# Attention kernel on one core: a local tile's sixteen exponentials issued as four steps, with the first stage ordered anew

## The chip, the core and the metric

One core of a Trainium2 chip runs the kernel. Its engines work through queues of their own, each strictly in the order in which the program was written, and wait for one another through semaphores: PE (TensorE) multiplies matrices and also transposes tiles, PEld is its weight load, DVE (VectorE), ACT (ScalarE) and POOL (GpSimd) work on elements, SP (SyncE) issues most of the DMAs. The metric is the device time of one execution in microseconds (us), lower is better.

## What is computed

`x` has 2 x 1024 tokens of 512 numbers. After a layer norm, two attentions are added to the input:

```python
xn = layernorm(x)
# local attention: 16 heads of 32, 4 key heads, RMS norm and RoPE on q and k
scores = einsum('bhqd,bhkd->bhqk', q, k) * scale
scores = where(causal | abs(i - j) > 64, -10000, scores)
a = einsum('bhqk,bhkd->bhqd', softmax(scores), v) @ Wo.T + bo
# routed attention: 16 heads of 32, one shared key and value per token,
# picked for each token by the largest of 16 gates; causal, not windowed
b = softmax(where(causal, q2 @ k_shared.T / sqrt(32), -inf)) @ v_shared
out = x + a + b
```

## The kernel before

**Two stages.** The first runs over 8 rounds of 256 tokens (two tiles of 128 each). It makes the projections of a round (`gemm`, L934 and L938) and the whole local attention. The second, from about 400 us on, is the routed attention (`key_scores`, `key_values`, `row_scores` and so on). 

**The plan sets the order.** `make_plan()` writes one list of steps, in the order in which a small model of the machine reaches them, and each engine's program walks through that one list and issues its own part of each step. So where a step stands in the list decides its place in every engine's queue. In the model the products (in *chunks* of three matmuls) are the filler: whenever no chain is due, the next chunk is placed. A chain is a generator; each `yield us, [(engine, us), ...]` says what its step costs on PE and on others, and the chain is due again when these have ended, plus `HOP` (0.2). Costs are booked when the yield is reached, so the model may book two steps on an engine in another order than they have in the list.

**The chain of a local tile** is `attend(m, a)` for round m and tile a. Its steps: `q_t` and `k_t` (transposes of q and k, copied by ACT, L1467 and L1475); `scores` (PE, into the four PSUM banks of `win`, L983 and L988); `maxima` (DVE, `l_max`, L1257); `weights` (ACT, sixteen exponentials from `win` into `p_loc`, L1492, four for each bank); `sums` (DVE, `l_sum` and `l_rec`, L1266 and L1269); `scaled` (POOL, `p_loc`, L1658); four `p_t` steps, one for each quarter of the queries (PE transposes of `p_loc` into one bank of `win`, L998, then an ACT copy to `p_loc_t`, L1501); `values` (PE, `av`, L1010); `attn` (ACT and DVE, `attn_t`, L1509 and L1274); `project` (PE, L1024), whose result DVE adds to `x_res` (L1283).

**The four banks are shared** by neighbouring tiles. The next tile's `scores` fill all four before this tile's `p_t` steps; the transposes of quarter g go to bank g, and may start when the next tile's exponentials have read bank g (`p_exp` counts these four by four). So a tile's `p_t` steps and the next tile's `weights` share ACT at the same time.

**Other names that matter.** `x_t` transposes the next round's input (L905), copied by ACT (L1411) and DVE (L1159, `xt`). `fk_lo` is a small DVE step (L1223, `fk_stack`), which `fk_stack` on PE waits for (L965). `qt` copies a routed-query product out of its bank (ACT L1460, DVE L1249). `q_rms` is POOL's L1610. The last two `qt` chunks (`LAST_CHUNKS`) are kept in the room of `rope_b` and `rope_sq`.

Of the kernel before, what the change touches and what calls it, by code (L numbers as in the profile page):

```python
# [179 lines left out]
def make_plan():  # L180
# [3 lines left out]
    pieces_made = [0]  # L184
    p.turned, p.transposed, p.projected, p.fk_stacked = set(), set(), set(), -1
    p.q_kept, p.av_free, p.rooms = -1, 0.0, False
    p.q_lands = {}

    win_free = [0.0] * HKV

# [118 lines left out]
    def take_q(n, kind, a, freed):  # L309
        do("q_biased", n, a)  # L310
        yield 0, [("V", 0.7)], freed
        do("q_square", n, a)
        p.busy(p.now, ("G", 5.2))
        yield 0, [("A", 0.75)]
        do("q_rms", n, a)
        do("q_rope", n, a)
        yield 0, [("V", 1.1), ("G", 3.6), ("G", 1.6), ("", SLACK)]
        yield from attend(n, a)

    def take_qt(n, kind, c, freed):  # L320
        do("qt", n, c)
        yield 0, [("A", 0.4), ("V", 0.45)], freed
        if c == 0 and n < S // PAIR:
            for _ in range(6):
                yield None
            p.q_kept = n
        if n == ROUNDS - 1 and c in (1, 2):
            quarter = 2 * (c - 1)
            do("q_load", 1, 0, 1, quarter)
            p.q_lands.update({(1, quarter + q): p.now + Q_LANDS for q in range(2)})  # L330

    def attend(m, a):
# [21 lines left out]
        yield 1.6, []  # L354
        do("maxima", m, a)
        yield 0, [("V", 1.75)]
        do("weights", m, a)
        def exps_end(end):
            win_free[:] = [end - 1.1 * (HKV - 1 - g) + HOP for g in range(HKV)]
        yield 0, [("A", 4.4)], exps_end  # L360
        do("sums", m, a)
        yield 0, [("V", 2.0)]
        do("scaled", m, a)
# [51 lines left out]
    def first_maxima():  # L415
# [22 lines left out]
            yield None  # L438
        p.take("tp1", ("max_in_rows", 0), ("r_lo", 0))
        do("max_in_rows", 0, 0)  # L440
        yield 0.11, [("A", 0.27)]
        do("max_low", 0, 0)
        yield 0, [("V", 0.35)]
        for _ in range(15):
            yield None

# [260 lines left out]
def mixed_attention_kernel(nc, counts, x, w_tok, w_qt, w_o, b_qkv, b_o, w_norm, scale, rope, ident, mask, rows, rank,  # L707
# [666 lines left out]
    def scalar_program(e):  # L1374
# [12 lines left out]
        for step, *key in plan.steps:  # L1387
# [94 lines left out]
                             tp1[0:HALVES, 0:2, :], ACT.Copy).then_inc(*M["fk_out"].did(m))  # L1482

            elif step == "weights":
                m, a = key
                lane.wait_ge(*M["s_max"].of((m, a)))
                if m:
                    lane.wait_ge(*M["pt_mm"].of((m - 1, a, QUADS - 1)))
                for g in range(HKV):
                    for quad in range(QUADS):  # L1490
                        n = g * QUADS + quad
                        i = e.activation(p_loc[a][:, g, quad, :], win[:, g, quad * KEYS:(quad + 1) * KEYS], ACT.Exp,  # L1492
                                         bias=l_max[:, a, n:n + 1])
                    i.then_inc(*M["p_exp"].did((m, a, g)))

            elif step == "p_t":
                m, a, quad = key
# [414 lines left out]
```

## Time and profile before

| | us |
|---|---|
| three timed runs | 684.29, 685.91, 686.01 |
| their median | 685.91 |
| span of the profiled execution | 684.4 |
| PE busy in it | 646.0 |
| span without PE busy | 38.4 |

How to read the rows further down. A row of the page's first part is an engine, its busy time, its share of the span and its instructions. A row by stretches gives from:to, its length, then busy time of PE, PEld, DVE, ACT and POOL (instructions in brackets), the granted clock of PE as a share of full speed, the busy share of the DMA engines and GB/s. A row of waits gives who waited, for whom, the total in us, how many times and the longest. A row of the timeline gives start, duration, engine, line, operation, output and input, shapes and how many instructions are merged in it; in square brackets how long the engine had idled before and what released it. Row starts of PE overlap with the end of the row ahead of them, because matmuls are pipelined.

### The profile page before, as it was taken

Reading aid. Unit: us, or ns where it says so; the run is one execution under the profiler, and the core shown is the slowest. Engines: PE = TensorE matmul, PEld = TensorE weight load, DVE = VectorE, ACT = ScalarE, POOL = GpSimd, SP = SyncE. Lnnn points to the kernel's source line nnn. Section 1 sums busy time; section 2 is a strip of 40 time slices with the busy share of each in tenths; the row PEclk is TensorE's granted clock in tenths of the full one; section 3 lists DMA queues with packets and bytes.
Section 4 is the critical chain, followed back from the end, with each engine's and each line's share of the span. In section 5 each row is a group of like instructions: output and inputs, shape, how many; then the busy total and the mean of one; then the engine's idle time right before and its main releaser. Section 6 shows DMA issues by size and latency. Waiting matters only on the chain.

```text
span 684.4 us, 19451 instructions
## 1 busy us (share of the span) xinstructions
PE 646.0 (94%) x7432; PEld 510.2 (75%) x7432; DVE 496.3 (73%) x1328; ACT 362.5 (53%) x906; POOL 442.6 (65%) x368
## 2 busy tenths in 40 slices
PE   3788999999999899999899899999999999999997
PEld 3577888887788688888688667777777777777775
DVE  3956966677678866787676368888888787879454
ACT  4436444472527344445335555556566566656674
POOL 3965764938195735684487267685868777778730
PEclk9979999999999999999999999999999999999999
DMA  8522213231232032222214541321314131402011
GB/s 295 206 59 86 82 38 115 86 98 51 66 102 61 30 112 70 64 70 74 77 32 118 158 142 56 96 64 50 111 49 110 51 106 32 110 28 87 4 33 33
DMA packets 64942, 56.61 MB, mean 83 GB/s; under 512 B 6481, under 2 KB 48849, under 8 KB 64849
## 3 DMA queue, kind: packets, MB, share of 16 engines
q1 hardware_dynamic: 62704, 54.45, 27.2%
q8 instruction: 58, 0.95, 0.6%
q10 hardware_dynamic: 2144, 0.93, 0.5%
q14 instruction: 36, 0.29, 0.1%
HBM read 37.20 MB, written 17.89 MB: 80 GB/s over the span
## 4 chain that ended last, share of the span: by engine, by line
PE 78%; DVE 9%; POOL 4%; ACT 3%; issue 2%; DMA 2%; ACTq 1%; DVEq 0%; POOLq 0%
PE gemm L938 17%; PE s_ps L1047 12%; PE od_ps L1096 11%; PE st_ps L1080 10%; PE gemm L1024 6%; PE od_ps L1110 5%; PE win L998 3%; PE gemm L934 3%; PE win L983 2%; PE s_ps L1119 2%; DMA rope_t<-rope 2%; PE av L1010 2%; DVE l_sum L1266 2%; ACT p_loc L1492 2%; DVE l_max L1257 1%
## 5 line engine op out<-in xcount | busy, mean ns | idle before, releaser
L938 PE MATMUL gemm<-w_tok,xt 128*128 128x512 f32 (+1 forms) x768 | 186.1, 384 | 3.3 <-DVE x_res L1283 0.9
L938 PEld LDWEIGHTS gemm<-w_tok,xt 128*128 128x128 f32 x768 | 131.7, 193 | 28.2 <-issue 1.4
L1318 DVE CUSTOM_DVE_ANT_0 s_ps<-s_ps,x_ln 128x512 f32<-128x512 f32 (+3 forms) x224 | 127.6, 620 | 24.4 <-PE s_ps L1047 24.0
L1047 PE MATMUL s_ps<-k_stack,w_tok 96*128 96x512 f32 (+2 forms) x336 | 101.5, 385 | 0.3 <-DVE x_res L1283 0.3
L1080 PE MATMUL st_ps<-w_tok,k_stack 98*128 98x512 f32 x288 | 99.0, 413 | 0.2 <-ACT p_loc L1540 0.2
L1540 ACT ACTIVATE p_loc<-st_ps 128x512 f32<-128x512 f32 x144 | 77.7, 599 | 36.0 <-PE st_ps L1080 34.8
L1634 POOL TENSOR_TENSOR rope_b<-qkv,sin_t 128x128 f32<-128x128 f32 (+1 forms) x32 | 27.5, 880 | 79.5 <-DVE qkv L1232 79.3
L1047 PEld LDWEIGHTS s_ps<-k_stack,w_tok 96*128 96x128 f32 x336 | 55.0, 188 | 28.3 <-DVE picked_fk L1318 12.4
L1492 ACT ACTIVATE p_loc<-win,l_max 128x96 f32<-128x96 f32 x256 | 60.9, 391 | 19.1 <-DVE l_max L1257 19.0
L934 PE MATMUL gemm<-xt,w_qt 128*128 128x256 f32 x384 | 57.1, 293 | 6.3 <-DVE picked_fv L1211 3.5
L1540 ACT ACTIVATE p_loc_t<-st_ps 128x512 f32<-128x512 f32 x96 | 52.4, 599 | 19.8 <-PE st_ps L1080 19.3
L1318 DVE CUSTOM_DVE_ANT_0 s_ps<-s_ps,x_ln,picked_fk 128x128 f32<-128x128 f32 (+3 forms) x112 | 56.8, 556 | 7.5 <-PE s_ps L1047 7.1
L1658 POOL TENSOR_TENSOR p_loc<-p_loc,l_rec 128x1536 f32<-128x1536 f32 x16 | 44.1, 2757 | 26.9 <-DVE l_rec L1269 26.9
L1610 POOL TENSOR_TENSOR rms_y<-rms_v,minus_half 128x20 f32<-128x20 f32 x16 | 58.6, 3665 | 3.3 <-DVE rms_v L1242 2.8
L934 PEld LDWEIGHTS gemm<-xt,w_qt 128*128 128x128 f32 x384 | 50.6, 194 | 10.2 <-DVE picked_fv L1211 4.5
L1024 PE MATMUL gemm<-w_o,attn_t 128*128 128x512 f32 x192 | 54.8, 414 | 3.2 <-DVE attn_t L1274 2.4
L1080 PEld LDWEIGHTS st_ps<-w_tok,k_stack 98*128 98x128 f32 x288 | 50.5, 189 | 9.0 <-ACT p_loc L1540 2.1
L1318 DVE DVE_READ_ACCUMULATOR2_ANT picked_fk<- 128x1 f32 x336 | 47.8, 142 | 0.0
L1501 ACT ACTIVATE p_loc_t<-win 96x512 f32<-96x512 f32 x64 | 36.8, 634 | 16.6 <-PE win L998 16.5
L1096 PE MATMUL od_ps<-p_loc,v_all 128*32 128x128 f32 x1152 | 44.3, 277 | 0.0
L1024 PEld LDWEIGHTS gemm<-w_o,attn_t 128*128 128x128 f32 x192 | 34.1, 193 | 10.0 <-issue 3.2
L1676 POOL TENSOR_SCALAR_AFFINE_SELECT p_loc<-p_loc 128x512 f32<-128x512 f32 x40 | 25.0, 634 | 24.8 <-ACT p_loc L1540 24.8
(172 smaller groups left out, 1298.7 us busy)
## 6 DMA issues: line engine op xcount, KB each, us to landing
w_tok<-q_parts SPq DMA_DIRECT2D x72, 128.0 KB, 2.6
q_parts<-qt SPq DMA_DIRECT2D x120, 64.0 KB
x_ln<-x SPq DMA_DIRECT2D x8, 512.0 KB, 4.7
x_res<-x SPq DMA_DIRECT2D x16, 256.0 KB, 2.9
partial<-x_res SPq DMA_DIRECT2D x16, 256.0 KB, 2.6
w_tok<-partial SPq DMA_DIRECT2D x8, 512.0 KB, 5.2
raw<-w_tok SPq DMA_DIRECT2D x3, 1024.0 KB, 12.9
v_win<-v_rows SPq DMA_DIRECT2D x64, 48.0 KB, 2.2
```

Source lines behind the costliest of these rows:

```text
L934: i = e.matmul(g[:, 0:PAIR], w_qt_p[r][:, k, a * P:(a + 1) * P], xs[l][:, k, :], start=first, stop=last)
L938: i = e.matmul(g[:, 0:cols], xs[l][:, k, a * P:(a + 1) * P], w_tok_p[r][:, k, c0:c0 + cols], start=first, stop=last)
L1024: i = e.matmul(gemm[bank][:, :], attn_t[l][:, kc, :], w_o_p[r][:, kc, :], start=kc == 0 and q == 0, stop=kc == KC - 1 and q == 2)
L1047: e.matmul(s_ps[bank][:, 0:cols], q_op[b][0:HALVES, i, h, :], k_stack[0:HALVES, b * S + c0:b * S + c0 + cols], start=True, stop=True).then ...
L1080: e.matmul(st_ps[k % ST_BANKS][:, :, :], k_stack[0:HALVES + 2, b * S + j * P:b * S + (j + 1) * P], q_op[b][0:HALVES + 2, i, :, :], start=T ...
L1096: mm = e.matmul(od_ps[h * DK:(h + 1) * DK, 0, :], v_all[:, b * IT + j, 0:DK], p_t[k % RING][:, h, :], start=i == j, stop=ends_row(k))
L1318: e.tensor_tensor_reduce(out=s[:, 0:cols], in0=s[:, 0:cols], in1=causal[:, S - width + c0:S - width + c0 + cols], scale=1.0, scalar=dst if ...
L1492: i = e.activation(p_loc[a][:, g, quad, :], win[:, g, quad * KEYS:(quad + 1) * KEYS], ACT.Exp, bias=l_max[:, a, n:n + 1])
L1501: e.activation(p_loc_t[quad][0:KEYS, :, :].rearrange("p g q -> p (g q)"), win[0:KEYS, quad, :], ACT.Copy).then_inc(*M["p_t_r"].did((m, a, ...
L1540: e.activation(p_t[k % RING][:, :, :], st_ps[k % ST_BANKS][:, :, :], ACT.Exp, scale=ROUTED_SCALE).then_inc(*M["rp_exp"].did((u, k)))
L1610: e.tensor_tensor(rms_y[:, :], rms_v[:, :], minus_half[:, :].to_broadcast([P, NH]), ALU.pow).then_inc(*M["rms_r"].did((n, a)))
L1658: e.tensor_tensor(p_l, p_l, l_rec[:, a, :].unsqueeze(2).to_broadcast([P, H, KEYS]), ALU.mult).then_inc(*M["p_r"].did((m, a)))
```

## The change

The `weights` step of a tile, one step of sixteen exponentials, becomes four steps `weights(m, a, g)` of four exponentials each, one for each score bank. On ACT the instructions, their operands and the semaphore counts stay as they were; other ACT work can now stand between the four. In the model each costs 1.1 us of ACT and ends with a hop, where the one step cost 4.4, and bank g is booked as free when step g is reached.

Two smaller edits go with it: the last two `qt` steps are held back until the last tile's rotation steps are in the list (they write into its rooms), and `max_low` follows `max_in_rows` at once. As the model's times differ, the order of the whole first stage is another one. The second stage's order is the same.

```diff
     def take_qt(n, kind, c, freed):
+        while (n, c) in LAST_CHUNKS and not p.roped:
+            yield None
         do("qt", n, c)
...
         do("maxima", m, a)
         yield 0, [("V", 1.75)]
-        do("weights", m, a)
-        def exps_end(end):
-            win_free[:] = [end - 1.1 * (HKV - 1 - g) + HOP for g in range(HKV)]
-        yield 0, [("A", 4.4)], exps_end
+        for g in range(HKV):
+            do("weights", m, a, g)
+            yield 0, [("A", 1.1)], lambda end, g=g: win_free.__setitem__(g, end + HOP)
         do("sums", m, a)
...
         do("max_in_rows", 0, 0)
-        yield 0.11, [("A", 0.27)]
         do("max_low", 0, 0)
-        yield 0, [("V", 0.35)]
+        yield 0.11, [("A", 0.27), ("V", 0.35)]
...
             elif step == "weights":
-                m, a = key
+                m, a, g = key
                 lane.wait_ge(*M["s_max"].of((m, a)))
                 if m:
                     lane.wait_ge(*M["pt_mm"].of((m - 1, a, QUADS - 1)))
-                for g in range(HKV):
-                    for quad in range(QUADS):
...
-                    i.then_inc(*M["p_exp"].did((m, a, g)))
+                for quad in range(QUADS):
+                    n = g * QUADS + quad
+                    i = e.activation(p_loc[a][:, g, quad, :], win[:, g, quad * KEYS:(quad + 1) * KEYS], ACT.Exp,
+                                     bias=l_max[:, a, n:n + 1])
+                i.then_inc(*M["p_exp"].did((m, a, g)))
```

What it moves is seen best on ACT at the first place where one tile's transposes meet the next tile's exponentials (`p_t` of tile 0,1 and `weights` of tile 1,0). Before:

```order
L1492 ACTIVATE p_loc0<-win,l_max 128x96 x16
L1411 ACTIVATE xt00<-tp1 128x4x128
L1501 ACTIVATE p_loc_t0<-win 96x512
L1501 ACTIVATE p_loc_t1<-win 96x512
L1501 ACTIVATE p_loc_t2<-win 96x512
L1501 ACTIVATE p_loc_t3<-win 96x512
L1449 ACTIVATE rope_sq<-qkv1 128x640
```

After:

```order
L1412 ACTIVATE xt00<-tp1 128x4x128
L1492 ACTIVATE p_loc0<-win,l_max 128x96 x4
L1501 ACTIVATE p_loc_t0<-win 96x512
L1492 ACTIVATE p_loc0<-win,l_max 128x96 x4
L1501 ACTIVATE p_loc_t1<-win 96x512
L1492 ACTIVATE p_loc0<-win,l_max 128x96 x4
L1501 ACTIVATE p_loc_t2<-win 96x512
L1492 ACTIVATE p_loc0<-win,l_max 128x96 x4
L1501 ACTIVATE p_loc_t3<-win 96x512
```

The four copies stood behind all sixteen exponentials; now each but the last stands ahead of the next bank's four. On PE at the same place, before (x3 is one chunk of 512 columns, x6 of 272 columns are two small ones):

```order
L998 MATMUL win<-idt,p_loc 96x128 x4
L938 MATMUL gemm<-w_tok,xt 128x272 x6
L998 MATMUL win<-idt,p_loc 96x128 x4
L938 MATMUL gemm<-w_tok,xt 128x272 x6
L998 MATMUL win<-idt,p_loc 96x128 x4
L938 MATMUL gemm<-w_tok,xt 128x512 x3
L998 MATMUL win<-idt,p_loc 96x128 x4
```

After:

```order
L999 MATMUL win<-idt,p_loc 96x128 x4
L939 MATMUL gemm<-w_tok,xt 128x512 x6
L999 MATMUL win<-idt,p_loc 96x128 x4
L939 MATMUL gemm<-w_tok,xt 128x512 x6
L999 MATMUL win<-idt,p_loc 96x128 x4
L939 MATMUL gemm<-w_tok,xt 128x512 x6
L999 MATMUL win<-idt,p_loc 96x128 x4
```

Between two quarters' transposes stood about one chunk; now there are two. The second place is the end of the first stage on ACT (`weights` of the last tile, `p_t` of the tile before it). Before:

```order
L1460 ACTIVATE rope_sq<-gemm0 128x256
L1492 ACTIVATE p_loc1<-win,l_max 128x96 x16
L1501 ACTIVATE p_loc_t0<-win 96x512
L1501 ACTIVATE p_loc_t1<-win 96x512
L1501 ACTIVATE p_loc_t2<-win 96x512
L1501 ACTIVATE p_loc_t3<-win 96x512
```

After:

```order
L1461 ACTIVATE rope_sq<-gemm0 128x256
L1492 ACTIVATE p_loc1<-win,l_max 128x96 x8
L1501 ACTIVATE p_loc_t0<-win 96x512
L1492 ACTIVATE p_loc1<-win,l_max 128x96 x4
L1501 ACTIVATE p_loc_t1<-win 96x512
L1492 ACTIVATE p_loc1<-win,l_max 128x96 x4
L1501 ACTIVATE p_loc_t2<-win 96x512
L1501 ACTIVATE p_loc_t3<-win 96x512
```

Two copies moved in between the last tile's exponentials. The third place is the start, on ACT, around the very first tile's exponentials. Before:

```order
L1492 ACTIVATE p_loc0<-win,l_max 128x96 x16
L1411 ACTIVATE xt01<-tp1 128x4x128
L1437 ACTIVATE fk_stack1<-chosen_fk 128x32
L1439 ACTIVATE fk_stack1<-chosen_fk 128x32
L1460 ACTIVATE qt0<-gemm0 128x256
```

After:

```order
L1492 ACTIVATE p_loc0<-win,l_max 128x96 x4
L1412 ACTIVATE xt01<-tp1 128x4x128
L1492 ACTIVATE p_loc0<-win,l_max 128x96 x4
L1438 ACTIVATE fk_stack1<-chosen_fk 128x32
L1440 ACTIVATE fk_stack1<-chosen_fk 128x32
L1461 ACTIVATE qt0<-gemm0 128x256
L1492 ACTIVATE p_loc0<-win,l_max 128x96 x4
```

The copy of the transposed input stands behind four exponentials instead of sixteen.

## Rows read from the trace of the kernel before

**Rows 1.** The page's first part, busy time by engine.

```profile
PE 646.0 (94%) x7432; PEld 510.2 (75%) x7432; DVE 496.3 (73%) x1328; ACT 362.5 (53%) x906; POOL 442.6 (65%) x368
```

**Rows 2.** Busy time by stretches: start, middle, end of stage one, stage two.

```profile
0.00:45.00 45.00, 28.29 (x116) 22.41 (x120) 27.79 (x45) 19.60 (x28) 26.59 (x27) 0.89 0.59 205
45.00:60.00 15.00, 12.42 (x117) 10.63 (x117) 11.05 (x14) 8.00 (x27) 10.35 (x8) 1.00 0.11 31
60.00:365.00 305.00, 296.08 (x2577) 247.54 (x2576) 224.21 (x426) 141.90 (x450) 193.62 (x137) 1.00 0.25 74
365.00:400.50 35.50, 30.84 (x298) 25.18 (x297) 13.71 (x23) 18.76 (x51) 15.66 (x13) 0.95 0.61 159
400.50:684.40 283.90, 278.34 (x4336) 204.48 (x4334) 219.55 (x823) 174.21 (x354) 196.40 (x186) 1.00 0.24 66
```

**Rows 3.** Waits of PE between 60 and 365 us.

```profile
PE tp L965 <- DVE fk_stack L1223: 3.5, 3, 1.8
...
PE tp L949 <- ACT k_stack L1481: 0.6, 1, 0.6
PE tp L956 <- ACT q_t L1467: 0.5, 1, 0.5
```

**Rows 4.** Timeline of PE, the transposes of tile 0,1.

```profile
86.54 0.60 PE L998 MATMUL win<-idt,p_loc 128*96 128x128 f32 x4
86.90 0.95 PE L938 MATMUL gemm<-w_tok,xt 128*128 128x512 f32 x3
87.69 0.60 PE L998 MATMUL win<-idt,p_loc 128*96 128x128 f32 x4
...
88.82 0.60 PE L998 MATMUL win<-idt,p_loc 128*96 128x128 f32 x4
...
89.97 0.60 PE L998 MATMUL win<-idt,p_loc 128*96 128x128 f32 x4
```

**Rows 5.** Timeline of ACT at the same place.

```profile
85.04 3.81 ACT L1492 ACTIVATE p_loc<-win,l_max 128x96 f32<-128x96 f32 x16
88.62 0.72 ACT L1411 ACTIVATE xt<-tp 128x512 fp32r<-128x512 f32 x1
89.09 2.11 ACT L1501 ACTIVATE p_loc_t<-win 96x512 f32<-96x512 f32 x4
```

**Rows 6.** Timeline: four transposes after a wait; a copy's transposes, and the copy.

```profile
77.65 0.66 PE L949 MATMUL tp<-idt,qkv 128*128 128x128 f32 x4 [0.26 <-POOL qkv L1618]
...
367.08 0.60 PE L998 MATMUL win<-idt,p_loc 128*96 128x128 f32 x4
...
367.72 0.59 ACT L1501 ACTIVATE p_loc_t<-win 96x512 f32<-96x512 f32 x1 [0.33 <-PE win L998]
```

**Rows 7.** Page, part 5: one exponential, 256 of them.

```profile
L1492 ACT ACTIVATE p_loc<-win,l_max 128x96 f32<-128x96 f32 x256 | 60.9, 391 | 19.1 <-DVE l_max L1257 19.0
```

**Rows 8.** Timeline of the end of stage one, ACT, DVE, POOL and PE.

```profile
377.79 3.80 ACT L1492 ACTIVATE p_loc<-win,l_max 128x96 f32<-128x96 f32 x16
381.35 2.11 ACT L1501 ACTIVATE p_loc_t<-win 96x512 f32<-96x512 f32 x4
...
381.90 0.69 DVE L1283 TENSOR_TENSOR x_res<-gemm,x_res 128x512 f32<-128x512 f32 x1 [3.56 <-PE gemm L1024]
382.51 1.74 DVE L1266 TENSOR_REDUCE l_sum<-p_loc 128x16 f32<-128x1536 f32 x1
...
383.52 1.08 PE L1010 MATMUL av<-p_loc_t,v_win 96*32 96x128 f32 x32 [0.78 <-ACT p_loc_t L1501]
384.62 2.76 POOL L1658 TENSOR_TENSOR p_loc<-p_loc,l_rec 128x1536 f32<-128x1536 f32 x1 [7.92 <-DVE l_rec L1269]
```

**Rows 9.** Timeline of round 5, POOL and DVE; a small DVE step.

```profile
235.64 2.75 POOL L1658 TENSOR_TENSOR p_loc<-p_loc,l_rec 128x1536 f32<-128x1536 f32 x1
...
236.25 2.19 DVE L1223 TENSOR_TENSOR fk_stack<-chosen_fk,fk_stack 128x32 fp32r<-128x32 f32 x1
```

**Rows 10.** Timeline of the start, around the first tile's exponentials.

```profile
52.70 0.63 PE L905 MATMUL tp<-idt,x_ln 128*128 128x128 f32 x4 [0.80 <-DVE xt L1159]
...
53.90 0.73 ACT L1411 ACTIVATE xt<-tp 128x512 fp32r<-128x512 f32 x1
...
56.00 1.31 PE L934 MATMUL gemm<-xt,w_qt 128*128 128x256 f32 x9 [1.29 <-DVE picked_fv L1211]
...
59.45 0.42 PE L965 MATMUL tp<-idt,fk_stack 128*96 128x128 f32 x2 [0.48 <-DVE fk_stack L1223]
```

**Rows 11.** PE by single microseconds: busy, granted clock, DMA share, GB/s.

```profile
388.00:389.00 1.00, 1.00 (x5) 0.50 0.29 86
```

More of the change, by code:

```diff
@@ L186, in make_plan @@
     p.q_kept, p.av_free, p.rooms = -1, 0.0, False
-    p.q_lands = {}
+    p.q_lands, p.roped = {}, False
     win_free = [0.0] * HKV
@@ L317, in take_q @@
         yield 0, [("V", 1.1), ("G", 3.6), ("G", 1.6), ("", SLACK)]
+        p.roped = (n, a) == LAST_TILE
         yield from attend(n, a)
     def take_qt(n, kind, c, freed):
+        while (n, c) in LAST_CHUNKS and not p.roped:
+            yield None
         do("qt", n, c)
@@ L1488, in scalar_program @@
                     lane.wait_ge(*M["pt_mm"].of((m - 1, a, QUADS - 1)))
-                for g in range(HKV):
-                    for quad in range(QUADS):
-                        n = g * QUADS + quad
-                        i = e.activation(p_loc[a][:, g, quad, :], win[:, g, quad * KEYS:(quad + 1) * KEYS], ACT.Exp,
-                                         bias=l_max[:, a, n:n + 1])
-                    i.then_inc(*M["p_exp"].did((m, a, g)))
+                for quad in range(QUADS):
[3 more added lines that the diff above has]
+                i.then_inc(*M["p_exp"].did((m, a, g)))
             elif step == "p_t":
```

## The prediction

> **What bounds the kernel now.** I read the page's first part first: PE is busy 646.0 of 684.4 us, DVE 496.3, POOL 442.6 and ACT 362.5 [rows 1]. The change adds no instruction, so PE's work stays what it is, and the time moves only by what is added to or taken from PE's 38.4 us of idle time. The view by stretches tells where that lies [rows 2]: 16.7 us before 45 us, where nothing of the order changes; 2.6 between 45 and 60; 8.9 between 60 and 365 (305.00 less 296.08); 4.7 at the end of the first stage; 5.6 in the second stage, whose order is unchanged. A better order of the first stage can therefore give back at most 2.6 + 8.9 + 4.7 = 16.2 us. The view of waits shows that little of it has to do with ACT: of the 8.9, ACT's copies released 0.6 and 0.5, and the largest item is DVE's small fk_stack step with 3.5 [rows 3]. What the split is good for, other ACT work that need not stand behind sixteen exponentials, has about 1.1 us to win there.
>
> **The main part: the loop that the new order closes.** Before, a tile's four groups of transposes start at 86.54, 87.69, 88.82 and 89.97 [rows 4], and no wait stands at any of them. They could run ahead of their copies, because ACT worked through the sixteen exponentials meanwhile (85.04, 3.81 us) and took the copies behind them [rows 5]. In the changed order copy g stands ahead of the exponentials of bank g+1, and the transposes of quarter g+1 write into bank g+1, so they wait for these exponentials. That is a closed loop through two engines: transposes g, copy g, four exponentials, transposes g+1. Its length in rows:
> - from the exponentials' end to the waiting PE: 0.06 (the copies end at 381.35 + 2.11 = 383.46, PE starts at 383.52 [rows 8]);
> - four transposes that start after a wait: 0.66 at 77.65, taken as 0.64 since most such rows without one show 0.60 [rows 6];
> - PE to ACT: 0.04 (367.08 + 0.60 to 367.72 [rows 6]);
> - the copy until ACT's next instruction starts: (2.11 - 0.60) / 3 = 0.50 [rows 5, 6];
> - four exponentials: one is 0.39 [rows 7] and sixteen take 3.81 [rows 5], so (3.81 - 0.39) / 15 = 0.228 from one to the next, and 3 x 0.228 + 0.39 = 1.07.
> Together 2.31 us from one group's start to the next. PE's own work between the two starts is, by the order, the transposes and two chunks in most places. One group and one chunk take 1.14 us (86.54 to 87.69, 87.69 to 88.82 [rows 4]); a chunk of 512 columns is 0.70 of that and the group 0.44, so with two chunks it is 0.44 + 2 x 0.70 = 1.84. PE must then stand still for 2.31 - 1.84 = 0.47 us. The plan didn't see this: its model books the four exponentials ahead of the copy, though the copy stands ahead of them in the list.
>
> **How many times.** I went through the 48 steps from one quarter to the next in the order of the changed kernel. 33 of them have the copy and the next bank's exponentials between them and so close the loop. In 16 of these PE has two chunks of work, or as much in smaller ones (1.84): 16 x 0.47 = 7.5 us. In ten others a small product comes on top, or a further ACT instruction stands in the loop (a square, 0.65, in tile 4,0; a small copy in tile 6,1), and they miss by 0.1 to 0.5, together 2.9. The other seven have 2.3 us or more of PE work and lose nothing. The sum is **10.4 us**, spread over 60 to 380 us. None of it has cover: what PE stands still for is on its own queue, and PE sets the end. From both sides: if the loop is 0.1 shorter than I put it, 26 places give 2.6 less (7.8); if it is 0.1 longer, 2.6 more (13.0).
>
> The Trainium skill (ScalarE: Activation LUTs, What ACT_TABLE_LOAD costs) gives an ACTIVATE with a pointer bias 280 ns + 0.833 ns for each element, and an overlap of 93 ns with the next one. For 96 elements that is 0.36 each, so 4 x 0.36 - 3 x 0.093 = 1.16 us for a group as an estimate from that page, 0.09 more than from the rows; the loop would be 2.40 and the sum 12.7. I keep the rows' value.
>
> **The end of stage one: +0.6.** The last tile's exponentials start behind the same copy (377.79 before [rows 8]), after the same amount of PE work. Two copies of 0.50 now stand between them, so they end at about 382.7 where they ended at 381.6. DVE took the sums at 382.51 only, because the addition to x_res stood ahead (381.90, 0.69 us [rows 8]). Now PE's last chunk there comes behind the third transposes and ends at about 382.4, the addition takes 0.6, and the sums start at 383.1. POOL's step (384.62 [rows 8]) and everything until the routed stage follow by that 0.6. The values of the tile before start 0.3 later, which is hidden under this chain.
>
> **The start: -1.1.** The copy of the transposed input ran at 53.90 behind the sixteen exponentials though its transposes were done at 52.70 + 0.63 = 53.33; it can now start at 53.37, and DVE's picked_fv, for which PE stood 1.29 at 56.00, comes some 0.6 earlier. fk_lo no longer stands behind the sums, which should clear the 0.48 at 59.45 [rows 10].
>
> **The middle's own waits: -3.** What PE waited for fk_stack is told by a row: a step of 32 columns took 2.19 us while POOL ran its 2.75 us step [rows 9]. Before, 0.7 to 2.7 us of PE work stood between fk_lo and PE's step; after, 0.8 to 2.7, and 1.7 or more in all rounds but one. I take 1.5 off the 3.5. The two ACT waits (1.1) go [rows 3]. Of the other 4.3 I take 0.4, since the loop gives DVE and POOL some ten more microseconds in the same stretch. The bounds: all 8.9 could go, or as much as 4 could come on top, if two more rounds meet POOL's step as the 2.19 did.
>
> **Sum.** 10.4 + 0.6 - 1.1 - 3.0 = **+6.9 us**. Against the profiled execution that is a span of 684.4 + 6.9 = 691.3; the median of the timed runs lies 1.5 above that span, so 685.9 + 6.9 = 692.8.
>
> **The rivals.**
> *Everything else pays (no change).* The loop binds as I say, but the new order clears the waits of the start and nearly all of the middle. Worked out: 10.4 + 0.6 - 2.6 - 8.9 = -0.5, with a shorter loop -3; so 683 to 688. For it speaks that the distance to fk_stack grows in most rounds. Against it speaks that waits such as DVE's order and POOL's long steps are not touched by the split.
> *The loop doesn't bind (faster).* If PE's work between the quarters were 2.3 us or more as it runs, because the chunks themselves wait there for something that the split then hides, the 10.4 would fall on waits that exist anyway, and only the gains remain: 0.6 - 1.1 - 3.0 = -3.5, so 682.4. It decides at 2.31 us between two transposes' starts. Against it: PE ran these stretches with no wait at all, at 1.14 for one chunk [rows 4].
> *New collisions, or the clock.* More rounds meet POOL's step in fk_lo (+2 each), or ACT stands at a copy for a late transpose with a `qt` or `xt` copy behind it that holds a PSUM bank. Beside it, the granted clock fell to 0.50, the 1.2 GHz level, at 388 after PE had idled for 1.5 and 0.4 us at the end of the stage [rows 8, 11]; a chunk that took 0.94 took 1.63 at that level. In the middle PE would be busy some 80% of the time in the loop's stretches, where no row shows a fall. Two or three such events give +4 to +6: 697 to 699.
> The Trainium skill (TensorE: Matmul & The Clock Gate, Part 1) names idleness as what halves this clock; the middle at 1.00 with 296 of 305 us busy and the fall at 388 agree with it, and by it the loop's stalls could bring a fall. I weigh that within the last rival.
>
> **How the numbers follow.** My forecast, 688.5 to 696.5, gets 0.64; new collisions 0.13; no change 0.14; faster 0.09. The range of 8 in 10 reaches from 686.0, into the case of no change, to 698.5, into the case of collisions. A measurement of this kernel can tell about 0.3%, or 2 us, from no change. Above 688.0 lie the forecast and the collisions, 0.77; between 683.9 and 688.0 0.15; below 0.08.
>
> **What would show it.** In the profile after, the waits of PE should have a new largest item, L999 (win<-p_loc) waiting for ACT's p_loc (L1492), some 25 to 30 times, 0.3 to 0.5 us each, 9 to 11 us in all, where there was none; the starts of the four transposes of tile 0,1 should be 2.3 us apart. PE's busy time stays at 646; between 60 and about 372 us its idle time rises from 8.9 to about 16. In the last stretch the sums start 0.6 us later after the exponentials' start than before. I am wrong if these waits are fewer than ten, if they are there and the waits for DVE vanish altogether, or if PE's clock leaves 1.00 in the middle.

## The result, and the profile after

| | before | after |
|---|---|---|
| median of four timed runs | 685.96 (684.29 to 687.57) | 698.93 (697.82 to 699.70) |
| span of the profiled execution | 684.4 | 698.5 |
| PE busy in it | 646.0 | 654.3 |

The ratio is 1.019 with a 95% interval of 1.0168 to 1.0212, so 13.0 us slower; I had forecast 6.9 us slower and a range up to 698.5. The profiled executions differ by 14.1.

The page's first part of after, to be read beside [rows 1]:

```profile
PE 654.3 (94%) x7432; PEld 512.1 (73%) x7432; DVE 503.7 (72%) x1328; ACT 366.7 (53%) x906; POOL 442.9 (63%) x368
```

PE has the same 7432 instructions but is busy 8.3 us longer. The forecast had this number unchanged. The stretches, beside [rows 2] (the same columns), and two short ones of the middle:

```profile
45.00:60.00 15.00, 13.37 (x122) 11.54 (x122) 10.36 (x18) 7.84 (x27) 9.78 (x7) 1.00 0.14 43
60.00:388.00 328.00, 312.49 (x2638) 256.80 (x2637) 236.56 (x430) 151.79 (x466) 198.82 (x140) 0.99 0.26 74
388.00:414.40 26.40, 22.13 (x229) 16.49 (x227) 9.47 (x14) 13.12 (x35) 11.08 (x8) 0.94 0.55 151
414.40:698.50 284.10, 278.29 (x4336) 204.95 (x4336) 219.70 (x825) 174.41 (x355) 196.64 (x186) 1.00 0.24 66
...
150.00:155.00 5.00, 4.02 (x40) 3.60 (x44) 1.14 (x2) 1.25 (x4) 1.99 (x2) 0.67 0.18 51
155.00:160.00 5.00, 5.00 (x41) 4.66 (x42) 2.87 (x5) 0.14 (x1) 0.00 (x0) 0.64 0.67 208
```

Stage two begins at about 414.4 where it began at 400.5 and takes 284.1 where it took 283.9, so all of the loss lies in the first stage. The start has 1.63 us idle where it had 2.58. In the middle the granted clock is 0.99, no longer 1.00, and the last two rows show where it fell: between 150 and 160 us PE ran for some 7 us at half clock, the 1.2 GHz level. At 0.67 and 0.64 over ten microseconds that is at most 5 x 0.33 + 5 x 0.36 = 3.5 us lost, and these show as busy time.

The waits of PE in the middle, beside [rows 3]:

```profile
PE tp L966 <- DVE fk_stack L1224: 5.7, 6, 1.7
PE win L999 <- ACT p_loc L1492: 3.3, 16, 0.2
PE tp L950 <- DVE w_tok L1330: 1.4, 1, 1.4
PE av L1011 <- DVE r_first L1300: 1.3, 2, 1.0
```

The wait that I forecast is there (second row), but it isn't the largest. The largest is the one for fk_stack, of which I had taken 1.5 us off; it grew from 3.5 us in three places to 5.7 in six.

**The loop.** Timeline of PE at the transposes of tile 0,1, beside [rows 4]:

```profile
91.95 0.64 PE L999 MATMUL win<-idt,p_loc 128*96 128x128 f32 x4 [0.20 <-ACT p_loc L1492]
92.35 1.65 PE L939 MATMUL gemm<-w_tok,xt 128*128 128x512 f32 x6
94.19 0.64 PE L999 MATMUL win<-idt,p_loc 128*96 128x128 f32 x4 [0.19 <-ACT p_loc L1492]
94.59 1.64 PE L939 MATMUL gemm<-w_tok,xt 128*128 128x512 f32 x6
96.43 0.64 PE L999 MATMUL win<-idt,p_loc 128*96 128x128 f32 x4 [0.20 <-ACT p_loc L1492]
```

And ACT there, beside [rows 5]:

```profile
92.63 0.60 ACT L1501 ACTIVATE p_loc_t<-win 96x512 f32<-96x512 f32 x1 [0.73 <-PE win L999]
93.13 1.01 ACT L1492 ACTIVATE p_loc<-win,l_max 128x96 f32<-128x96 f32 x4
94.87 0.60 ACT L1501 ACTIVATE p_loc_t<-win 96x512 f32<-96x512 f32 x1 [0.73 <-PE win L999]
95.37 1.01 ACT L1492 ACTIVATE p_loc<-win,l_max 128x96 f32<-128x96 f32 x4
```

From 94.19: transposes 0.64, to the copy 0.04, copy until the next start 0.50 (94.87 to 95.37), four exponentials 1.01, back to PE 0.05 (96.38 to 96.43). The loop is 2.24 us long. PE's own work between two starts was 1.84 by [rows 4], and it is 1.82 in the run with the loop opened (below), so some 0.4 is lost at each turn here. The row of waits shows only half of that as idle (0.20), because the ends of a run of matmuls are modelled. For the real loss I took the time from each PE step's start to the next step's, in both traces, against the lower quartile of that kind of step. Between 60 us and the last chunk of the first stage (377.0 before, 391.3 after) this gives:

| time lost on PE ahead of | before | after |
|---|---|---|
| transposes of p_loc | 0 | 7.7 in 25 places |
| fk_stack | 4.3 in 4 | 7.2 in 6 |
| half clock at 151 to 160 | 0 | 3.5 |
| q_t | 1.2 | 2.2 |
| everything else | 24.4 | 24.7 |

Together 15.4 more, less some 1.0 won at the start (idle 2.58 to 1.63): 14.4, where the spans differ by 14.1. The entries are estimates and depend on how the steps are sorted into kinds.

**The collision.** Rounds are numbered here as in the code, from 0. DVE, POOL and PE in round 2, rows picked from the timeline (beside [rows 9]):

```profile
145.90 1.74 DVE L1267 TENSOR_REDUCE l_sum<-p_loc 128x16 f32<-128x1536 f32 x1
...
147.84 0.63 DVE L1212 TENSOR_TENSOR picked_fv<-gemm,g_hot 128x512 f32<-128x512 f32 x1
148.01 2.75 POOL L1658 TENSOR_TENSOR p_loc<-p_loc,l_rec 128x1536 f32<-128x1536 f32 x1
...
148.51 1.07 DVE L1217 TENSOR_REDUCE chosen_fv<-picked_fv 128x32 f32<-128x512 f32 x1
...
149.49 1.32 DVE L1224 TENSOR_TENSOR fk_stack<-chosen_fk,fk_stack 128x32 fp32r<-128x32 f32 x1
...
150.86 0.42 PE L966 MATMUL tp<-idt,fk_stack 128*96 128x128 f32 x2 [1.72 <-DVE fk_stack L1224]
```

In the new order the sums stand directly ahead of picked_fv and fk_lo. The sums release POOL's scaling at 148.01; DVE reaches fk_lo 1.5 us later, in the middle of it, and fk_lo ends at 150.81, just after POOL (150.76). It is so in rounds 1, 2, 3, 5 and 6; in round 4 fk_lo meets POOL's step on qkv (640 columns) and ends with that. From round 1 to 6 fk_lo takes 1.29, 1.32, 0.99, 1.10, 1.08 and 2.35 us, where the kernel before has 0.18, 0.96, 0.18, 2.19, 0.18 and 2.29. The fall of the clock comes right behind this wait.

### The profile page after: what moved, and what is told of

It is laid out like the page before. It is cut to its first block, busy times and chain, and to the rows that moved or that the text cites. A ratio compares the mean times of both kernels' runs of the same rounds, so it can differ in the third digit from the quotient of the medians.

```text
span 698.5 us, 19445 instructions
## 1 busy us (share of the span) xinstructions
PE 654.3 (94%) x7432; PEld 512.1 (73%) x7432; DVE 503.7 (72%) x1328; ACT 366.7 (53%) x906; POOL 442.9 (63%) x368
## 4 chain that ended last, share of the span: by engine, by line
PE 72%; DVE 12%; ACT 5%; issue 4%; POOL 3%; DMA 2%; ACTq 0%; DVEq 0%; POOLq 0%
PE gemm L939 13%; PE s_ps L1048 11%; PE od_ps L1097 11%; PE st_ps L1081 10%; PE gemm L1025 6%; PE od_ps L1111 5%; PE win L999 4%; PE win L984 3%; DVE l_sum L1267 3%; ACT p_loc L1492 3%; PE s_ps L1120 2%; PE gemm L935 2%; DMA rope_t<-rope 2%; ACT p_loc_t L1501 2%; PE av L1038 1%
## 5 line engine op out<-in xcount | busy, mean ns | idle before, releaser
L1319 DVE CUSTOM_DVE_ANT_0 s_ps<-s_ps,x_ln 128x512 f32<-128x512 f32 (+3 forms) x224 | 127.3, 618 | 24.4 <-PE s_ps L1048 24.1
L1492 ACT ACTIVATE p_loc<-win,l_max 128x96 f32<-128x96 f32 x256 | 64.8, 345 | 30.9 <-DVE l_max L1258 30.9
L935 PE MATMUL gemm<-xt,w_qt 128*128 128x256 f32 x384 | 59.3, 298 | 5.3 <-DVE g_exp L1181 2.8
L935 PEld LDWEIGHTS gemm<-xt,w_qt 128*128 128x128 f32 x384 | 52.1, 198 | 10.1 <-DVE g_exp L1181 4.0
L999 PE MATMUL win<-idt,p_loc 128*96 128x128 f32 x256 | 40.0, 279 | 3.8 <-ACT p_loc L1492 3.3
```

The lines of the kernel that those rows point to most:

```text
L935: i = e.matmul(g[:, 0:PAIR], w_qt_p[r][:, k, a * P:(a + 1) * P], xs[l][:, k, :], start=first, stop=last)
L999: i = e.transpose(win[0:KEYS, quad, g * P:(g + 1) * P], p_loc[a][:, g, quad, :], idt[:, :])
L1319: e.tensor_tensor_reduce(out=s[:, 0:cols], in0=s[:, 0:cols], in1=causal[:, S - width + c0:S - width + c0 + cols], scale=1.0, scalar=dst if ...
```

## The experiments

Times are set against the kernel before on the same chip. A ratio less one, times 686, gives the microseconds behind it; the changed kernel's is +13.0. The expectations use 698.9 as its time.

| run | edit on | ratio (95%) | us |
|---|---|---|---|
| e1_ahead | after | 1.0148 (1.0110 to 1.0186) | +10.2 |
| e2_undo | after | 1.0167 (1.0139 to 1.0195) | +11.5 |
| e3_fk_early | after | 1.0283 (1.0248 to 1.0318) | +19.4 |
| e4_rows_late | after | 1.0176 (1.0147 to 1.0206) | +12.1 |
| e5_lo_in_sums | after | 1.0098 (1.0070 to 1.0125) | +6.7 |
| e6_both | after | 1.0006 (0.9989 to 1.0024) | +0.4 |
| e7_one_input | after | 1.0091 (1.0069 to 1.0114) | +6.2 |
| e8_three | after | 1.0014 (0.9999 to 1.0028) | +1.0 |
| c2_replanned_both | after | 1.0124 (1.0097 to 1.0150) | +8.5 |
| b1_fk_early | before | 0.9944 (0.9921 to 0.9967) | -3.8 |
| b2_split_start | before | 0.9992 (0.9977 to 1.0007) | -0.5 |
| b3_start_and_fk | before | 0.9935 (0.9912 to 0.9957) | -4.5 |

The intervals are 1 to 2.6 us to either side, so a difference between two of these kernels is known to some 2 to 3 us. Of each kernel one execution is traced, and the granted clock of a whole execution differs between executions of one kernel (0.985, 0.985, 0.992 and 0.992 for the changed one). Where the clock fell is therefore known for the traced execution only.

### The loop opened

The edit moves steps in the finished list, and nothing is planned anew:

```diff
+def open_loop(steps):
+    for m in range(1, 2 * ROUNDS):
+        tile, ahead = divmod(m, 2), divmod(m - 1, 2)
+        for g in range(HKV - 1):
+            p_t, weights = steps.index(("p_t", *ahead, g)), steps.index(("weights", *tile, g + 1))
+            if steps.index(("weights", *tile, 0)) < p_t < weights:
+                steps.insert(p_t, steps.pop(weights))
```

> The changed kernel's list with one thing moved: the exponentials of bank g+1 stand ahead of the transposes of quarter g (33 steps moved by one place), so ACT's order is exponentials 0, exponentials 1, copy 0, exponentials 2, copy 1 and so on. Everything else stands where it stood. The loop theory: the 25 stalls of PE at the transposes of p_loc, 7.7 us in all between 60 and 388 us, vanish, since a group of transposes no longer waits for exponentials that stand behind the copy of the group before. Time 698.9 - 7.7 = 691.2 (690 to 692.5). The half clock at 150 to 160 us, which follows a wait of 1.72 us for fk_stack, stays. Rival one, the clock follows from the loops (PE less busy ahead of 150): the half clock vanishes too, 3.4 us more, 687.8. Rival two, the stalls only took the room of other waits (DVE's and POOL's chains set the pace of a round): the waits for DVE grow by what the loop gives back and the time stays at 696 or more.

PE's timeline of tile 0,1 in this kernel:

```profile
90.71 0.60 PE L1010 MATMUL win<-idt,p_loc 128*96 128x128 f32 x4
91.06 1.62 PE L950 MATMUL gemm<-w_tok,xt 128*128 128x512 f32 x6
92.53 0.60 PE L1010 MATMUL win<-idt,p_loc 128*96 128x128 f32 x4
```

The groups are 1.82 apart, no wait stands at them, and of the 7.7 us at the transposes 0.3 is left. The loop is real and is the mechanism of these stalls. But the time falls by only 2.8 us, not by 7.7, and by the two intervals even the 2.8 carries an error of some 3. The other half of the trace says why. Its waits, and its stretches of low clock:

```profile
PE tp L977 <- DVE fk_stack L1235: 6.9, 5, 1.7
```

```profile
148.00:156.00 8.00, 7.88 (x73) 7.27 (x74) 2.45 (x5) 1.25 (x4) 1.06 (x1) 0.59 0.48 137
288.00:296.00 8.00, 6.94 (x78) 6.63 (x79) 3.50 (x7) 2.19 (x6) 2.20 (x2) 0.79 0.40 96
338.00:344.00 6.00, 4.45 (x38) 3.91 (x28) 3.20 (x4) 1.95 (x5) 2.94 (x2) 0.72 0.15 43
```

PE arrives earlier at fk_stack and waits 6.9 for it instead of 5.7, and the clock now falls three times instead of once: 8 x 0.41 + 8 x 0.21 + 6 x 0.28 = 6.6 us where it was 3.5. So 7.4 won, 1.2 and 3.1 given back: 3.1. The first rival (the loops cause the fall of the clock) is refuted, since there are more falls without them; the granted clock was 0.983 in all four executions of this kernel, lower than in any of the changed one. The second (PE only waits elsewhere) is half right.

The other way to open the loop puts all four groups of exponentials ahead of the first transposes:

```diff
+        for g in range(1, HKV):
+            p_t, weights = steps.index(("p_t", *ahead, 0)), steps.index(("weights", *tile, g))
+            if steps.index(("weights", *tile, 0)) < p_t < weights:
+                steps.insert(p_t, steps.pop(weights))
```

> The changed kernel's list with the split undone on ACT alone: all four groups of exponentials of a tile stand ahead of the first transposes of the tile before it, as in the kernel before; PE, DVE and POOL keep the order of the changed kernel. The loop theory: the same as with the exponentials one bank ahead, 691.2 (690 to 692.5), since neither order closes the loop. The rival, that ACT's finer interleaving is itself worth something (values, av and copies earlier): this one is 1 us or more slower than the order with one bank ahead. A second rival, that all of the 13 us comes from the split on ACT: 686.

It came out 1.3 us above the one with the exponentials one bank ahead, with intervals that overlap. In it the clock falls twice in the middle, near 150 and near 340. So with the split on ACT undone, but the new order elsewhere, 11.5 of the 13.0 us stay: the larger part of the loss is not ACT's.

### fk_lo out of POOL's way

The first try moved fk_hi and fk_lo ahead of whichever of the sums and picked_fv comes first:

```diff
+        made = steps.index(("picked", n, "fk", 1))
+        to = min(k for k in (steps.index(("sums", n, 0)), steps.index(("picked", n, "fv", 1))) if k > made)
+        for step in (("fk_hi", n, 1), ("fk_lo", n, 1)):
+            if steps.index(step) > to:
+                steps.insert(to, steps.pop(steps.index(step)))
+                to += 1
```

> The changed kernel's list with fk_hi and fk_lo of the second tile in rounds 1 to 6 moved ahead of the next sums or picked_fv, whichever comes first. The loops stay. Collision theory: fk_lo then runs before POOL's scaling of p_loc begins and takes 0.18 us, not 1.0 to 2.35; PE's six waits for fk_stack, 5.7 us, shrink to under 1 (-5), and with the wait of 1.72 us at 150.86 the half clock between 151 and 160 us vanishes, another 3.4. Time 698.9 - 8.4 = 690.5 (689 to 692). Rival: the half clock comes from the loop's stalls and stays: 694. Rival: sums and scaling start 0.5 later in each round and the transposes behind them become the wait: 696 or more.

A clear miss: 6 us slower than the changed kernel instead of 8 faster. DVE's timeline of round 3 in it shows why:

```profile
188.79 0.19 DVE L1236 TENSOR_TENSOR fk_stack<-chosen_fk,fk_stack 128x32 fp32r<-128x32 f32 x1 [2.74 <-ACT fk_stack L1450]
188.90 1.75 DVE L1279 TENSOR_REDUCE l_sum<-p_loc 128x16 f32<-128x1536 f32 x1
...
190.85 0.34 DVE L1312 CUSTOM_DVE_ANT_0 av<-av,diagonal,r_first 128x128 f32<-128x128 f32 x1
```

and PE's:

```profile
191.39 1.08 PE L1023 MATMUL av<-p_loc_t,v_win 96*32 96x128 f32 x32 [1.89 <-DVE r_first L1312]
```

fk_lo takes 0.19 as wanted in five of the six rounds, but ACT's fk_hi stands behind the last exponentials, and DVE's queue stands 2.74 us for it (4.23 in round 1) with the sums and r_first behind it. PE waits 4.7 us for r_first instead of 1.3 and 3.0 for picked_fv instead of 0.8, and the clock falls twice, behind a wait of 2.44 for r_first and one of 1.87 for picked_fv. The wait was moved, not removed. The traced execution was the shortest of the four (701.8; the others took 705.3 to 705.7 at a lower granted clock).

The second try puts fk_lo between the two instructions of the sums, where POOL can't have started, since it waits for the second one, and where ACT has had 1.7 us for fk_hi:

```diff
+        if 0 < n < ROUNDS - 1 and steps.index(("picked", n, "fk", 1)) < steps.index(("sums", n, 0)):
+            for step, last in (("fk_hi", ("sums", n, 0)), ("fk_lo", ("rec", n, 0))):
+                if steps.index((step, n, 1)) > steps.index(last):
+                    steps.remove((step, n, 1))
+                    steps.insert(steps.index(last), (step, n, 1))
...
+            elif step == "rec":
```

> The changed kernel with DVE's fk_lo of rounds 1 to 6 put between l_sum and l_rec of the sums (ACT's fk_hi directly ahead of these sums), so that it runs before POOL's scaling of p_loc can start, and DVE does not stand for ACT. The loops stay. Collision theory: fk_lo takes 0.18 us, PE's six waits for fk_stack (5.7 us) go, and the half clock at 150 to 160 us, which followed the longest of them, goes too (3.4 us): 698.9 - 5.7 - 3.4 = 689.8 (688.5 to 691.5). Rival, what stands still is DVE's queue as a whole, and PE waits for its next item (picked_fv, r_first, qt) in fk_stack's place: 695 or more, the half clock still there.

DVE and POOL in round 1 of this kernel:

```profile
94.82 1.75 DVE L1281 TENSOR_REDUCE l_sum<-p_loc 128x16 f32<-128x1536 f32 x1 [2.80 <-ACT p_loc L1509]
96.49 0.18 DVE L1238 TENSOR_TENSOR fk_stack<-chosen_fk,fk_stack 128x32 fp32r<-128x32 f32 x1
96.60 0.25 DVE L1287 RECIPROCAL l_rec<-l_sum 128x16 f32<-128x16 f32 x1
...
96.94 2.76 POOL L1675 TENSOR_TENSOR p_loc<-p_loc,l_rec 128x1536 f32<-128x1536 f32 x1 [2.40 <-DVE l_rec L1287]
```

6.3 us faster than the changed kernel, expected 9.1. No half clock is left between 60 and 381 us (the granted clock there is 1.00). Of the missing 2.8 us, 1.6 is at fk_stack: PE still waits 0.78 in two rounds, now for ACT's copy of q_t, which had been hidden behind fk_lo. The edit clears POOL's scaling but not POOL's step on qkv (640 columns): beside that one fk_lo still took 0.38 in round 2 and 1.00 in round 5, and PE did not wait for it.

The third try moves nothing and changes fk_lo's form. The low part of fk is left out, and a copy of chosen_fk stands in its place; the wait for fk_hi stays:

```diff
-                e.tensor_tensor(dst[:, 2 * DK:3 * DK].bitcast(F32R), chosen["fk"][:, :], dst[:, 0:DK],
-                                ALU.subtract).then_inc(*M["fk_lo"].did((n, a)))
+                e.tensor_reduce(dst[:, 2 * DK:3 * DK].bitcast(F32R), chosen["fk"][:, :].unsqueeze(2), AX.X,
+                                ALU.max).then_inc(*M["fk_lo"].did((n, a)))
```

> The changed kernel with one instruction in another form: fk_lo is a reduction over one element with one input (chosen_fk) where it was a subtraction of two inputs in SBUF; the low part of fk is left out thereby (it becomes a copy), nothing is moved. It separates what holds fk_lo beside POOL's scaling. If it is the second input in SBUF: fk_lo takes 0.2 us in all six rounds though POOL still runs beside it, PE's waits for fk_stack fall from 5.7 to about 0.6, the half clock at 150 to 160 us goes, and the time is 698.9 - 5.1 - 3.4 = 690.4 (689 to 692.5). If any small DVE instruction on SBUF is held by POOL's: fk_lo keeps its 1.0 to 2.35 us and the time stays 698 to 700.

Round 2 of it, the same place as above:

```profile
145.74 2.76 POOL L1658 TENSOR_TENSOR p_loc<-p_loc,l_rec 128x1536 f32<-128x1536 f32 x1
...
147.22 0.18 DVE L1224 TENSOR_REDUCE fk_stack<-chosen_fk 128x32 fp32r<-128x32 f32 x1
...
147.46 0.42 PE L966 MATMUL tp<-idt,fk_stack 128*96 128x128 f32 x2 [0.58 <-DVE fk_stack L1224]
```

POOL's step is still running, the DVE instruction stands where it stood, and it takes 0.18 instead of 1.32. 6.8 us of the 13.0 are gone, with no half clock in the middle. So half of the loss hangs on the form of one instruction of 32 columns. The edit changes two things of it, the number of its inputs in SBUF and the operation (a reduction in place of a subtraction). That it isn't the subtraction is told by rows of the changed kernel shown in the last section, in which one with an input in PSUM is not held. The Trainium skill (SBUF — State Buffer, SBUF: two separate sides) says that a DVE operation with two inputs in SBUF and a GpSimd operation that reads SBUF share a pair of ports, which the one that starts first holds for its whole instruction. This run agrees with it for POOL's multiplication of 128x1536 (2.76 us); beside POOL's power of 128x20 the traces do not (last section).

### Both together

> The same, and the loop opened as in the run with the exponentials one bank ahead. If the 13 us are the sum of three things, loop stalls 7.4, collisions of fk_lo with POOL 2.9 to 4 over the kernel before, and the half clock that follows PE's waits 3.4 to 6.7, then this kernel gets nearly all of it back: 698.9 - 7.4 - 5.7 - 3.4 = 682.4 (681 to 685), no slower than the kernel before. Rival, the pace of a round is set by DVE's and POOL's chains in this order, whatever PE waits for by name: 690 or more, with the clock falling in the middle again.

1.0006: the changed kernel with these two edits is as fast as the kernel before, 686.4 by the ratio. That is 4 us above the 682.4 expected and outside the range of that expectation: PE waits 3.2 us for r_first where it waited 1.3 in the changed kernel, and 1.7 for q_t's copy at fk_stack. Between 60 and 376 us:

```profile
60.00:376.00 316.00, 306.21 (x2678) 256.77 (x2681) 232.66 (x432) 150.72 (x466) 199.25 (x141) 1.00 0.27 77
```

The four kernels make a square. Opening the loop brings 2.8 us while fk_lo collides and 6.3 once it doesn't; taking away the collision brings 6.3 with the loops and 9.8 without. The steps of 6.3, 9.8 and the 12.6 of both together are clear of the intervals. Singly the two edits bring 2.8 + 6.3 = 9.1; the 3.5 between this and 12.6 carries an error of nearly 4 us, so that the causes do more together than singly is suggested, not shown. In the traces 3.1 us of two further falls of the clock, in the run with the open loop alone, stand for it.

### The end of stage one

```diff
-        while not p.rooms:
+        while not p.rooms or LAST_TILE not in p.turned:
             yield None
```

> The changed kernel with max_in_rows and max_low held back until the last tile's q and k are transposed, as they stood before; only steps behind about 383 us change their place. Theory: the wait of 1.44 us at 385.15, where q_t of the last tile waits for max_low to release its PSUM bank, vanishes and everything behind it comes 1.4 to 1.7 earlier: 697.3 (696.8 to 698). Rival: the last tile's chain waits for something else by then (POOL's rotation, ACT's order) and the time stays within 0.5 of 698.9.

0.9 us faster, less than the two intervals can tell, and the wait of 1.44 is gone from the trace; a wait of 0.46 for ACT's copy of k_t came in its place. On top of the other two edits it brought nothing:

> The changed kernel with the loops opened, fk_lo inside the sums, and max_in_rows held back until the last tile is transposed. The first two gave 687.0, level with the kernel before; the third alone gave 0.8 to 1.5. If the three add up: 1 us below the kernel before (ratio 0.9985, 0.996 to 1.001), with PE's time between 60 us and the end of the first stage's last product back at that of the kernel before. Rival: with the loops open q_t of the last tile waits for POOL's rotation anyway and nothing is gained: ratio 1.0005 to 1.002.

1.0014, the rival's number. With the loops open q_t waited only 0.6 us there, and the 0.5 for k_t takes its place.

### The planner mended

```diff
-            yield 0, [("A", 1.1)], lambda end, g=g: win_free.__setitem__(g, end + HOP)
+            yield 0, [("A", 1.1), ("", -HOP)], lambda end, g=g: win_free.__setitem__(g, end + 2 * HOP)
```

This comes with the two edits of the list (open loop, fk_lo in the sums).

> A candidate: the planner's chain resumes at the end of a bank's exponentials and not a hop later, so the next bank's exponentials come into the list ahead of the transposes, and the whole first stage is planned with it; what loops are left (19 places) are opened in the list, and fk_lo stands inside the sums. By the theory of loops, collisions and clock: no stall at the transposes of p_loc, no wait for fk_stack above 0.3, no half clock between 60 and 380 us, 681 to 686. Rival (pace by DVE and POOL): as the run before, 690 or more.

A miss, 8.5 us slower than before. There is one wait of 1.5 at the transposes, at the end of the stage (388.73), and none for fk_stack, but this is a third order of the whole stage with waits of its own. The largest wait of PE between 60 and 387 us, and the longest of its stretches of low clock:

```profile
PE gemm L958 <- DVE picked_fv L1235: 5.4, 5, 2.0
```

```profile
262.00:268.00 6.00, 3.76 (x27) 3.16 (x25) 5.90 (x10) 0.86 (x3) 5.86 (x4) 0.89 0.00 0
268.00:276.00 8.00, 7.79 (x60) 6.17 (x61) 1.73 (x8) 2.56 (x6) 1.33 (x3) 0.50 0.38 104
```

Whether an order comes out with DVE's work ahead of PE's need is not in the model's hands here: it books neither the collision nor the clock.

### The same finding on the kernel before

> The kernel before with fk_hi and fk_lo of the second tile in rounds 1 to 6 moved ahead of picked_fv. In it fk_lo took 2.19 and 2.29 us in two rounds beside POOL's scaling of p_loc, and PE waited 4.0 us for fk_stack in four places. Collision theory: these waits go, 3 us net, 682.5 (681.5 to 683.5). Rival, as in the first try on the changed kernel: DVE stands for ACT's fk_hi ahead of picked_fv, what PE gains at fk_stack it loses at picked_fv, 685 to 687.

The code is that of the first try. In this order picked_fv comes first in five of the six rounds, and DVE has to stand for fk_hi only in round 2 (1.3 us). PE's waits between 60 and 369 us begin with

```profile
PE gemm L946 <- DVE picked_fv L1223: 1.3, 3, 0.5
PE av L1022 <- DVE r_first L1311: 1.1, 2, 0.9
```

and fk_stack isn't among them. 3.8 us faster than before, so this beats both kernels without any split. One part of the change alone, the split of the very first tile's exponentials (the fourth group behind x_t's copy, fk_lo ahead of the sums):

> The kernel before with one part of the change alone: only the very first tile's exponentials are split, the fourth group behind the copy of the transposed input (x_t of round 1), and fk_lo of round 0 ahead of the sums. Nothing else moves. Theory of the start: the copy runs at 53.37 instead of 53.90, PE's wait of 1.29 for picked_fv shrinks to about 0.7 and the 0.48 for fk_stack goes: 1.0 us faster than the kernel before (0.5 to 1.5). Rival: the microsecond is lost again behind, since the next waits (DVE's qkv, x_t) come that much earlier: within 0.3.

The trace shows the microsecond at its place: the product that started at 56.00 behind 1.29 us of wait [rows 10] starts at 55.34.

```profile
55.34 1.31 PE L943 MATMUL gemm<-xt,w_qt 128*128 128x256 f32 x9 [0.64 <-DVE picked_fv L1220]
```

In time it is 0.5 us with an interval from 1.6 faster to 0.5 slower, which can't be told from nothing. In this profile the clock fell at 332 us, which it didn't in that of the kernel before. Both edits together:

> The kernel before with the split at the start and fk_hi and fk_lo ahead of picked_fv, a candidate. The one gave 4.0 us; if the two add up, it is 5 us faster than the kernel before (ratio 0.993, 0.991 to 0.995). Rival: as above, the start's gain is lost: ratio 0.9945.

0.9935, 4.5 us faster than before, the fastest kernel of this study, though not measurably faster than the one with fk_lo alone.

## Where the prediction was right and where it was wrong

- **Direction and place: right.** Slower, in the first stage alone, with PE waiting for exponentials at the transposes. The time after, 698.93, is just outside the range; the third rival (new collisions, or the clock: 697 to 699), which I gave 0.13, is what happened, on top of the loop. That its number fits is in part luck: it priced collisions at +2 each and the loop at 10.4.
- **The loop: right, the term mis-sized.** 2.31 us was 2.24 (four exponentials took 1.01 for 1.07), so 0.40 for each full turn and not 0.47; 25 places and not 26, of which not all lose a full turn; 7.7 us and not 10.4. The figures of the Trainium skill that I set beside it (ScalarE: Activation LUTs, What ACT_TABLE_LOAD costs) would by that estimate have made the group 1.16, where the trace has 1.01, and went further off. What 7.7 us of stall are worth in time, the runs put at 2.8 to 6.3, with some 3 us of error. The view of waits showed 16 waits of 0.20, so "25 to 30 times, 0.3 to 0.5 each" can't be read off it.
- **The start: right.** -1.1 forecast, about -1.0 in the trace: the wait for picked_fv fell from 1.29 to 0.64 and the 0.48 for fk_stack went, while one of 0.20 for k_stack came.
- **The end of stage one: right for the sums, worth nothing.** The sums started 4.72 us behind the exponentials' start before (377.79 to 382.51 [rows 8]) and start 5.39 behind it after, +0.67 where I had +0.6:

```profile
392.14 1.96 ACT L1492 ACTIVATE p_loc<-win,l_max 128x96 f32<-128x96 f32 x8
...
397.53 1.74 DVE L1267 TENSOR_REDUCE l_sum<-p_loc 128x16 f32<-128x1536 f32 x1
```

  But stage two begins 22.3 us behind the exponentials' start in both. The four groups of transposes behind it took 4.3 us from first to last and not 5.0, as the half clock of this place covered fewer of them. I had not seen the 1.44 us wait for max_low ahead of it.
- **The middle's own waits: the step that failed.** I took 3.0 off; they rose by 4.2 (fk_stack 2.9, q_t 1.0, others 0.3). I judged fk_stack by PE's work between fk_lo and PE's step, which did grow. What decides is when DVE reaches fk_lo relative to POOL's scaling, and that stood in the order too: in the old list the sums of tile (n,0) come ahead of picked_fk in five of six rounds, in the new one behind it and shortly ahead of fk_lo in all. From [rows 8] POOL starts 0.4 behind the end of the sums (384.25 to 384.62); l_rec and picked_fv take 1.8 (147.67 to 149.49); so fk_lo falls some 1.5 us into a step of 2.75. I had the row that shows what this costs [rows 9] and allowed for two more rounds as a bound; there were three more, six where the kernel before has three.
- **The clock: seen as a rival, not priced in.** 3.5 us in the changed kernel. I had asked whether the loop's stalls bring it; the traces speak for PE's longer waits for DVE: it is gone in the two kernels in which POOL's scaling doesn't hold fk_lo and nothing else waits much longer (fk_lo in the sums, one input), with the loop stalls in place; there are three falls where the loops are open and fk_lo is held, two where all exponentials stand ahead and fk_lo is held, and two where PE waits for r_first and picked_fv instead. The kernel before shows that such a wait can also pass without a fall (below).
- **PE busy 646: wrong.** Of the 8.3 us more, 3.5 are the half clock, and some 4 (7.7 less the 3.3 that the waits show) the part of the loop stalls that counts as busy.
- **The sum.** In the traces it is 7.7 (loop) + 0 (end of the stage) - 1.0 (start) + 4.2 (middle) + 3.5 (clock) = 14.4, where I had 10.4 + 0.6 - 1.1 - 3.0 + 0 = 6.9. The loop was put too high; the middle's waits, 7.2 us off and with the wrong sign, and the clock are what failed.

Open: why the clock fell at one wait and not at another. In the kernel before PE waited 1.79 us for fk_stack at 238.5, and the clock stayed full:

```profile
236.00:240.00 4.00, 2.21 (x14) 1.54 (x13) 2.91 (x5) 0.38 (x1) 3.64 (x2) 1.00 0.18 50
```

Four microseconds of the changed kernel around its wait of 1.72 look much the same (PE busy 2.16 for 2.21), and the fall came at their end:

```profile
148.00:152.00 4.00, 2.16 (x17) 1.73 (x15) 3.11 (x4) 1.36 (x3) 3.98 (x2) 0.97 0.01 4
```

Nor was it settled why opening the loop brought two more falls.

## What to carry to other kernels

When one engine's in-order queue takes turns between a producer and a consumer that share a buffer, write the loop down with all its members and compare it with the work in between; moving the next producer one place ahead of the consumer opens it. When an order is planned anew, look beyond the distances on the critical engine: list for each short instruction that it waits for what stands ahead of it in its own queue, and which instruction of another engine those very steps release. Stalls of one microsecond can have a price beyond their own length when the clock falls behind them, so mending one cause alone may pay less than its own stalls (here 2.8 of 7.7 us).

## What the runs showed of the hardware

A DVE subtraction of 128x32 with both inputs in SBUF takes 0.18 us alone and 0.99 to 2.35 in the changed kernel beside POOL's 2.75 us multiplication of 128x1536, always ending with it; the same columns with one input, as a reduction, take 0.18 beside it. Three rows of the changed kernel, POOL and DVE between 224 and 228 us, tell more of what is held:

```profile
224.34 2.76 POOL L1658 TENSOR_TENSOR p_loc<-p_loc,l_rec 128x1536 f32<-128x1536 f32 x1
...
224.55 0.41 DVE L1250 TENSOR_TENSOR qt<-gemm,qt 128x256 fp32r<-128x256 f32 x1
...
225.15 1.98 DVE L1153 TENSOR_SCALAR ln_v<-moments 128x2 f32<-128x2 f32 x1
```

The subtraction for qt has one input in PSUM (gemm) and takes the 0.41 that it takes elsewhere. The addition of a constant for ln_v, two columns and one input in SBUF, takes 1.98 and ends with POOL's step, where it takes 0.17 with POOL idle. So two inputs in SBUF are not the only form that is held; which property of ln_v's form does it was not tested.

Nor does every long POOL instruction hold fk_lo: beside the power of 128x20, which runs 3.53 us, the same subtraction took 0.19, though that power too reads SBUF (POOL and DVE in the first fk_lo try, round 4):

```profile
236.92 3.53 POOL L1622 TENSOR_TENSOR rms_y<-rms_v,minus_half 128x20 f32<-128x20 f32 x1
```

```profile
237.79 0.19 DVE L1236 TENSOR_TENSOR fk_stack<-chosen_fk,fk_stack 128x32 fp32r<-128x32 f32 x1 [0.49 <-ACT fk_stack L1450]
```

And a wait of PE that ends a run of matmuls shows only partly in the view of waits: the loop's 0.40 us show as 0.20.
